# Self attention: when the gated copies and the mixed-row additions of a step are done

## What is computed

```python
q = (x @ Wq).reshape(b, t, h, dh).transpose(0, 2, 1, 3)      # 4 batches, 512 rows, 8 heads of 64
k = (x @ Wk).reshape(b, t, h, dh).transpose(0, 2, 1, 3)
gl_v = (x @ Ws).reshape(b, t, h, e)                          # 5 experts, 2 chosen for each head and row
wv = _topk_mask(gl_v, SEL) * jax.nn.sigmoid(gl_v)
xv = jnp.einsum('btd,edk->btek', x, Wv)
v = jnp.einsum('bthe,btek->bhtk', wv, xv)
probs = jax.nn.softmax(jnp.einsum('bhid,bhjd->bhij', q * scale, k), axis=-1)
attn = jnp.einsum('bhij,bhjd->bihd', probs, v)
mask_o = _topk_mask((x @ Wd).reshape(b, t, h, e), SEL)
out = jnp.einsum('bthe,bthk,ekd->btd', mask_o, attn, Wo)
```

## Time and profile before

| | us |
|---|---|
| median of three runs | 2502.98 (2502.49 to 2504.49) |
| the profiled execution, its own time | 2505.09 |
| its span in the trace | 2503.3 |
| the self attention in it, from its first score products to its end | about 2061 to 2503 |
| TensorE busy in 2063 to 2495, of 432.0 | 378.2 |
| VectorE busy there | 333.0 |
| ScalarE busy there | 203.5 |
| mean granted TensorE clock there | 0.82 of full |

### The profile page before, as it was taken

One profiled execution on the slowest core, in us unless ns is written; L12 is line 12 of the kernel. 1 busy time (PEld: TensorE's weight loads), 2 busy tenths in 40 slices (PEclk: granted clock), 3 DMA queues, 4 the chain that ended last, 5 costly groups with the idle time before them and its releaser, 6 DMA issues. The chain is left out here.

```text
span 2503.3 us, 35267 instructions
## 1 busy us (share of the span) xinstructions
PE 2331.0 (93%) x13184; PEld 1499.1 (60%) x13184; DVE 1675.0 (67%) x2846; ACT 1189.4 (48%) x1896; POOL 922.8 (37%) x535
## 2 busy tenths in 40 slices
PE   4999999999999889799999999999999868889897
PEld 3555665655665578565566556655655456556665
DVE  4998798799888666545544554455455447878794
ACT  4666456456555320245543554455345413444454
POOL 3522222222122010176765775666567611001010
PEclk9999999999999989799999999999999977888887
DMA  4000000100010031300000000000000010000000
GB/s 114 20 1 26 18 1 1 43 1 1 1 60 1 2 88 43 86 13 1 1 26 18 1 1 26 18 1 1 1 26 1 1 54 9 1 1 26 18 1 26
DMA packets 62650, 48.65 MB, mean 19 GB/s; under 512 B 12242, under 2 KB 61970, under 8 KB 62482
## 3 DMA queue, kind: packets, MB, share of 16 engines
q1 hardware_dynamic: 62484, 46.40, 6.1%
HBM read 38.01 MB, written 8.39 MB: 19 GB/s over the span
## 5 line engine op out<-in xcount | busy, mean ns | idle before, releaser
L437 POOL TENSOR_TENSOR cross_acc_pool<-cross_acc_pool,cross_probs 128x1024 f32<-128x1024 f32 x186 | 443.6, 2385 | 44.5 <-ACT cross_probs L541 24.1
L660 DVE TENSOR_REDUCE cross_part<-cross_ring 128x1 f32<-128x512 f32 x512 | 324.1, 684 | 140.1 <-PE cross_ring L812 140.0
L423 POOL TENSOR_TENSOR latent_KR<-latent_rot 128x256 f32<-128x256 f32 x128 | 172.7, 1349 | 562.2 <-DVE latent_rot L654 562.2
L541 ACT ACTIVATE cross_probs<-cross_scores 128x1024 f32<-128x1024 f32 x256 | 250.0, 1025 | 101.9 <-PE cross_scores L845 99.6
L541 ACT ACTIVATE latent_probs<-latent_scores 128x1024 f32<-128x1024 f32 x256 | 247.2, 1017 | 74.9 <-PE latent_scores L841 74.9
L688 DVE TENSOR_TENSOR latent_acc_dve<-latent_acc_dve,latent_probs 128x1024 f32<-128x1024 f32 x192 | 258.9, 1349 | 10.4 <-DVE latent_acc_dve L688 0.5
L861 PE MATMUL latent_outT<-latent_probs,latent_VN 128*64 128x512 f32 x1024 | 247.9, 605 | 4.0 <-DVE latent_probs L675 3.9
L861 PE MATMUL cross_outT<-cross_probs,cross_VN 128*64 128x512 f32 x1024 | 248.0, 605 | 0.0
L675 DVE TENSOR_SCALAR latent_probs<-latent_probs 128x2048 f32<-128x2048 f32 x128 | 157.9, 1234 | 25.3 <-ACT latent_probs L541 25.3
L1152 POOL TENSOR_TENSOR self_acc_pool<-self_probs 128x1024 f32<-128x1024 f32 x16 | 39.3, 2456 | 350.0 <-ACT self_probs L1214 350.0
L733 PE MATMUL latent_ring<-latent_WH,latent_CTH 128*128 128x256 f32 x512 | 156.2, 305 | 1.1 <-DVE latent_newt L709 1.1
(11 more groups left out here) (303 smaller groups left out, 5606.3 us busy)
## 6 DMA issues: line engine op xcount, KB each, us to landing
C<-in_ctx_dram SPq DMA_DIRECT2D x8, 1024.0 KB, 6.9
XN<-x_after SPq DMA_DIRECT2D x12, 512.0 KB, 4.5
x_after<-X SPq DMA_DIRECT2D x10, 512.0 KB, 2.9
X<-x_after SPq DMA_DIRECT2D x10, 512.0 KB, 4.0
XN<-in_x_dram SPq DMA_DIRECT2D x4, 512.0 KB, 3.9
WRAW<-in_L_xattn_Wq_dram SPq DMA_DIRECT2D x16, 128.0 KB, 2.6
WRAW<-in_L_xattn_Wkv_dram SPq DMA_DIRECT2D x16, 128.0 KB, 2.6
X<-in_x_dram SPq DMA_DIRECT2D x4, 512.0 KB, 3.8
```

Of the source, the lines that this page charges most:

```text
L423: nc.gpsimd.tensor_tensor(KR[:, 2 * t:2 * t + 2, :], rot1s[n % 2][:, :, :], rot2s[n % 2][:, :, :], ALU.add)\
L437: nc.gpsimd.tensor_tensor(acc_pool[:, :, :], first[:, :, :], probs[g % PROBS][:, :, :], ALU.add)\
L541: nc.scalar.activation(probs[g % PROBS][:, :, :], scores[g % 2][:, :, :], ACT.Exp, scale=SCALE)\
L660: nc.vector.reduce_max(part[:, qt, h, i:i + 1], bank[:, :], AX.X).then_inc(taken, 1)
```

## The change

Four entries of the list move, and "mix" is split into its two additions, which become items of their own:

- The bundle on ScalarE for tile 0 goes from quarter 1, right behind "back", to the end of quarter 2.
- VectorE's copy for tile 3 of step s-2 goes from quarter 0 to the end of quarter 1, right ahead of the first addition.
- VectorE's copy for tile 1 goes from the `tail` to the `late` list of quarter 2.
- The second addition of a step goes from quarter 1 to the end of quarter 2.

No instruction is added or removed, and the waits stay the same ones, each with its instruction.

```diff
--- before.py
+++ after.py
@@ -909,14 +909,13 @@
             put(tail, s, 2, ("q", s + 2))
         if s:
             front[s * parts].insert(0, ("recip", s - 1))
-            put(tail, s, 1, ("back", s - 1), ("mask", s - 1, 0))
-            put(tail, s, 2, ("mask", s - 1, 1))
+            put(tail, s, 1, ("back", s - 1))
+            put(late, s, 2, ("mask", s - 1, 1), ("mask", s - 1, 0))
             put(late, s, 3, ("mask", s - 1, 2))
-        if s > 1:
-            put(late, s, 0, ("mask", s - 2, 3))
         put(late, s, 0, ("add", s, 1))
         if s > 1:
-            put(late, s, 1, ("mix", s - 2))
+            put(late, s, 1, ("mask", s - 2, 3), ("mix", s - 2, 0))
+            put(late, s, 2, ("mix", s - 2, 1))
         put(before, s, 2, ("add", s, 3))
         if p == 0 and more:
             put(front, s, 0, ("load", b + 1))
@@ -959,8 +958,8 @@
         plan += front[n + 2] + before[n + 2] + tail[n + 2] + late[n + 2]
         plan += front[n + 3] + [("AV", s, 2), ("AV", s, 3), ("evac", s)] + before[n + 3] + tail[n + 3] + late[n + 3]
     last = steps - 1
-    plan += [("recip", last), ("back", last), ("mask", last - 1, 3), ("mix", last - 1)]
-    plan += [("mask", last, t) for t in range(QT)] + [("mix", last)]
+    plan += [("recip", last), ("back", last), ("mask", last - 1, 3), ("mix", last - 1, 0), ("mix", last - 1, 1)]
+    plan += [("mask", last, t) for t in range(QT)] + [("mix", last, 0), ("mix", last, 1)]
     plan += [("mixT", B - 1, t) for t in range(QT)] + [("out", B - 1, t) for t in range(QT)] + [("store", B - 1)]
     return plan
 
@@ -1406,18 +1405,19 @@
                                             .broadcast_to([P, EXPERTS, 2, DH]), ALU.mult).then_inc(rows_gated, 1)
                 elif kind == "mix":
 
-                    s = item[1]
+                    _, s, h = item
                     b, p = divmod(s, NP)
                     by = mixed[b % 2][:, :, 0:NV].rearrange("p t (e k) -> p t e k", e=EXPERTS)
-                    if p == 0 and b >= 2:
-                        dve.wait_ge(full, unit["mixT", b - 2, QT - 1] + 1)
-                    dve.wait_ge(rows_masked, 2 * (s + 1))
-                    dve.wait_ge(rows_gated, 2 * (s + 1))
-                    if s:
-                        dve.wait_ge(mix_steps, mix_before[s])
-                    nc.vector.tensor_tensor(by, by if p else masked[s % 2][:, :, :, 1, :], masked[s % 2][:, :, :, 0, :], ALU.add)\
-                      .then_inc(mix_steps, 1)
-                    if p:
+                    if h == 0:
+                        if p == 0 and b >= 2:
+                            dve.wait_ge(full, unit["mixT", b - 2, QT - 1] + 1)
+                        dve.wait_ge(rows_masked, 2 * (s + 1))
+                        dve.wait_ge(rows_gated, 2 * (s + 1))
+                        if s:
+                            dve.wait_ge(mix_steps, mix_before[s])
+                        nc.vector.tensor_tensor(by, by if p else masked[s % 2][:, :, :, 1, :], masked[s % 2][:, :, :, 0, :], ALU.add)\
+                          .then_inc(mix_steps, 1)
+                    elif p:
                         dve.wait_ge(mix_steps, mix_before[s] + 1)
                         nc.vector.tensor_tensor(by, by, masked[s % 2][:, :, :, 1, :], ALU.add).then_inc(mix_steps, 1)
                 elif kind == "out":
```

## The result

| | before, us | after, us |
|---|---|---|
| median of the runs | 2502.73 | 2484.0 (2481.88 to 2488.49) |
| the profiled execution, its own time | 2505.09 | 2481.88 |
| its span | 2503.3 | 2480.1 |

The ratio is 0.9925, with a 95% interval of 0.9913 to 0.9937: 0.75% faster, 19 us.

What follows compares the result with a forecast made beforehand. TensorE, busy 93% of the span, was taken as the bound, with stalls and low clock in self attention. 13 + 9.2 + 0.8 - 1.2 = 21.8 us off 2505.1 gives 2483.3 profiled, median 2481, range 2474 to 2490.

Steps and rivals of the forecast that it cites:

- four releasers: TensorE's idle time in self attention: reciprocal 11.8 us, `XTL` 9.7, `mixedT` copies 7.2, maxima 6.8.
- The bundle in p = 1: Steps 1, 5, 9: `XTH` starts earlier; gains of 5, 4 and 4 us, together 13, between 7.2 and 15.
- the stall goes and the clock gives nothing: Lower bound for steps 1, 5 and 9: only the stall ahead of `XTL` is saved, 2.4 us each.
- rival 1: Stalls go but the clock gives nothing back, pauses remain in steps 5 and 9: gain 15.5 us, 2487.5; chance 0.17.
- The bundle in p = 2: Steps 6, 10, 14: `mixedT` copies start earlier; 3.1 us each, 9.2 in all, between 7 and 11.
- The bundle's new place: Bundle ahead of `OT` on ScalarE: costs nothing; up to 2.5 us a step if the cover were gone.
- The copy of tile 3: VectorE's copy no longer blocked by GpSimd's addition: 0.3 us saved in step 4, 0.5 in step 8, together 0.8.
- The warning by the Trainium skill's rule: Step 14: the moved copy comes to lie under GpSimd's addition and could cost up to 0.5 us.
- The second addition: Steps 4 and 8: the 1.86 us wait for a maximum goes but returns at the step's end; counted as zero.
- The costs: Steps 2, 3, 12, 13: VectorE reaches the reciprocal later, 0.3 us each, 1.2 in all; none in 7 and 11.
- Rival 2: VectorE takes the gain back, reciprocal late by 1 to 1.5 us in ten steps: gain about 10, 2493; chance 0.1.
- Rival 3: Longer low-clock stretches at step starts, 1.7 us at each of 15 boundaries: 10 us slower, 2513; chance 0.03.

Runs made afterwards that it cites:

- e9: The changed kernel with VectorE's copy of tile 3 ahead of `XTL` in quarter 1, in the p = 1 steps alone: 2480.64 us, ratio 0.9907.
- e12: The kernel before, with ScalarE's bundle moved in the p = 2 steps alone (2, 6, 10, 14): 2490.18 us, ratio 0.9942.
- e3: The changed kernel with both additions together in quarter 1, as before the change: 2484.39 us, ratio 0.9932.
- e1: The kernel before with only ScalarE's bundle moved; VectorE's copies and additions stay in their old places: 2482.3 us, ratio 0.9923.
- e4: The changed kernel with VectorE's copy of tile 3 back in quarter 0, the additions still split: 2476.36 us, ratio 0.9898.
- e10: e9 with VectorE's copy of tile 3 back in quarter 0 in the p = 2 steps: 2480.44 us, ratio 0.9905.
- e2: The kernel before with only VectorE's moves; ScalarE's bundle stays in its old place: 2500.35 us, ratio 1.0.
- e7: e4 with the first addition also at the end of quarter 2 in the p = 1 steps: 2479.15 us, ratio 0.9905.
- e8: e7 with VectorE's last gate operations of steps 2, 6 and 10 behind the next step's reciprocal: 2485.06 us, ratio 0.9928.
- e6: The kernel before with one "max" product issued ten more times where TensorE waits for `XTL` in steps 1, 5 and 9: 2500.9 us, ratio 0.9989.

## Why the prediction was right, point by point

*The time.* 2481 was forecast, 2484.0 measured, inside 2474 to 2490; by the profiled execution 2483.3 was forecast and 2481.9 measured, of which 3.4 us had been won ahead of step 1 by nothing that was changed. So the sum was 2 us too large over the steps (21.8 against 19.8) and 3 by the medians. That it came so near is in part luck: the two terms of the bundle were 4.8 us too large, and 3.5 us came in steps 4, 8 and 12 and behind step 14, where little or nothing was entered.

*The reading.* The list of four releasers left out two waits as large as those it names, for `QL` (10.1) and for the last addition (8.7). It did no harm: 9.15 of the first is the one at the start of the self attention, the second lies in the tail, and the changed kernel has both unchanged (9.13 and 8.7).

*The bundle in p = 1: 13 forecast, 9.7 measured.* The mechanism held as written: `XTH` at once, the "max" product 3.2 us earlier within step 5 (21.0 us behind the step's start before, 17.75 after). Step 1 gave 6.06, where 5 was taken. The mis-sized part is the clock in steps 5 and 9. The 4 us there took a good part of full clock for granted; step 5 gave 3.37, by the low bound of 3.2, and step 9 only 0.28, below every bound given. The bound "the stall goes and the clock gives nothing" was no bound. In step 9 the low stretch moved later, from where TensorE waited for VectorE anyway onto attention, gate and sum products. The pauses of rival 1 stand ahead of it in all traces (see above); which of them decides is not shown. With the copy ahead of `XTL` (e9) step 9 takes 26.71, 3.6 less than before, but its attention products are at half clock too.

*The bundle in p = 2: 9.2 forecast, 7.7 measured*: two of the three at the lower bound of 2.35 (2.25, 2.40), one where it was expected (3.04). In e12, where VectorE's order is the old one, the same three give 10.9. So the mechanism was worth more than forecast, and in these traces VectorE's moves took 3.2 us of it. In steps 6 and 10 TensorE waits 1.19 and 1.18 us for `QL` with the copy in quarter 1 (e3 too, 1.19), and 0.76 with the copy in quarter 0 (e1, e4, e10, e12): the copy's new place costs 0.4 there, and the prediction had no such loss for them. In step 14 e12 is 1.7 us shorter, and e3, with the copy in its new place, 1.5: there the changed kernel's clock is low for the first 6.7 us of the step, e12's and e3's for the first 3.5 or so, and what prolongs it is open.

*The bundle's new place costs nothing.* Right. ScalarE's wait in front of `OT` fell from 40.2 us to 10.0, and nothing waited for `OT`.

*The copy of tile 3.* That it would no longer be blocked was right: all copies from step 2 to 13 took 0.81 or 0.82. It had been blocked in nine steps before, with 1.08 to 1.54 us, and not only in the two that were counted; in e2, with VectorE's other moves beside it, this brought nothing in the sum. Step 4's gain from `KL` to the reciprocal was 0.2, step 8's 0.5, as forecast (0.3, 0.5); the rest of their 2.5 came ahead of `KL`, where the mean granted clock was 0.68 and 0.69 after 0.63 and 0.66, which explains a part of it. The warning by the Trainium skill's rule (SBUF — State Buffer, "Who interferes with whom") for step 14 came true: the copy fell under GpSimd's addition and took 2.22 us, ending 0.69 behind that addition's end at 2423.69. With the first mixed-row addition right behind it, which was held in its place before (2.46 us behind a copy of 0.82, and 1.49 behind this one), the loss is 0.4 us.

```profile
2421.30 2.39 POOL L1151 TENSOR_TENSOR self_acc_pool<-self_probs 128x1024 f32<-128x1024 f32 x1 [19.10 <-ACT self_probs L1213]
...
2422.16 2.22 DVE L1402 TENSOR_TENSOR self_masked<-self_natural,self_scaled 128x640 f32<-128x640 f32 x1
```

The step that failed is the sign of this part. It was entered as a gain of 0.8. The 0.75 us that the copy puts between `XTL` and `QL` was in the working, and the product behind `QL` came just when it was forecast (3.2 us earlier); but it was set off against the addition that left, and never priced as the cost of this move. It delays the bank of the second turned product and `QL` in steps 5 and 9 and `QL` in steps 6 and 10. By the ratios e4, with the copy back in quarter 0, is 7 to 8 us faster than the changed kernel, and e9, with it ahead of `XTL` in p = 1 alone, 4 to 6, the latter within overlapping intervals.

*The second addition.* Its zero in steps 4 and 8 held: most of TensorE's 1.86 us moved to the end of the step, where it waits 1.08 in front of "shift" and 1.99 for the reciprocal in step 4 (none and 1.76 before). e3 has no difference in the median, and in its steps 4 and 8 the time from `KL` to the reciprocal is 17.7 us, 17.6 in the changed kernel; that both steps are a microsecond longer there comes ahead of `KL`.

*The costs.* Steps 2, 3 and 13 lost 0.2 to 0.3 each as forecast. Step 12 won instead. Steps 7 and 11 lost 0.46 each where nothing was entered.

*The rivals.* Rival 1 describes steps 5 and 9, and no others. Rival 2 is out: the wait for the reciprocal grew by 0.9 us in all. Rival 3 appears once, at the end of step 9, where the clock is low from 2.2 us ahead of the reciprocal on. What holds step 9's low stretch in just that place in both traces of the changed kernel (30.06 and 30.03) is open. None of the kernels without a pause of 1.25 or more for a maximum there (e4, e7, e8, e9, e10) shows a step 9 as long, but e4, e9 and e10 too have half clock on its attention products (3.5, 3.4 and 3.3 us) and are still 3.2 to 3.4 us shorter.

## What to carry to other kernels

Ask of an engine in order what it does right before the instruction that another engine waits for. A bundle with a reader a step away, issued ahead of copies with a reader waiting, cost some 19 us here, and moving one list entry gave it back. When such a stall goes, look at everything between the freed instruction and the next buffer it frees: a further 0.8 us put there, beside the split additions, took back a quarter to a third of what e4 gains. The fastest of those measured is e4: bundle late, additions split, VectorE's copy where it was, 2476.4 us, 1.0% under the kernel before; e7, e9 and e10 can't be told from it.

## What the runs showed of the hardware

A full clock behind a stall is not time by itself: e6 filled 2.3 us of each of three waits with repeated products, the granted clock stayed at 2.4 GHz for 11 us behind it in step 1 and for 6.3 and 5.7 us in steps 5 and 9, and only step 1 became shorter. And low stretches move: step 4 of e6, with not one line different, took 2.33 us more than in the kernel before.

A VectorE multiplication or addition of two SBUF operands that began while GpSimd's addition of 2.4 us ran was held until that had ended, not slowed. All nine held copies of the kernel before, that of step 14 in the changed one and the 3.02 us one in step 14 of e4 end 0.67 to 0.69 us behind the end of GpSimd's addition, whether they began 0.2 us into it or in its last 0.4 us; a free copy takes 0.81. In e8 an addition of 0.69 took 2.77 and ended 0.54 behind it. Reductions from PSUM took 1.28 for two beside it as without it.
